# Vision tower kernel: the order of the first microseconds, from the taps' transfer to the second gray picture

## Chip, cores and metric

One core of one Trainium2 chip. The metric is device time in microseconds of one execution. Three runs of the kernel before gave a median of 251.41 us (251.34 to 252.23).

## What is computed

Eight images of 3x256x256 are each turned to gray and convolved with two 3x3 Scharr filters; the mean of the two absolute answers is a matrix of 256x256 per image, whose rows are the tokens. One attention head with biases and a causal mask follows, a residual and a layernorm, then a layer of 8 experts (top 1, at most 320 tokens each) with a residual and a layernorm.

```
gray  = einsum('bchw,c->bhw', x, (0.2989, 0.587, 0.114))
edges = conv(gray, scharr (2 filters), padding='SAME')
h     = (|edges_x| + |edges_y|) / 2                      # [8, 256, 256]
h     = layernorm(h + softmax(mask(Q K^T / 16)) V)       # Q, K, V = h W^T + b
h     = layernorm(h + moe(h, Wr, W1, W2))                # 8 experts, relu, capacity 320
```

## The kernel before, in words

All five engines run their own hand-written programs, ordered by semaphores (`wait_ge`, `then_inc`). Precision is kept by splitting each operand into a high half, rounded by ScalarE to fp32r, and a low half, the rest, which VectorE makes; a product is then three matmuls (high x high, high x low, low x high).

**Setup.** VectorE writes a row of ones and a block of ones (L905, L906, `still_ready`). The 18 taps come by a DMA from ScalarE's queue (L747), TensorE spreads them over 128 partitions (L1444), VectorE scales them (L908, `half_taps`). From them the banded matrices `band[dx, f]` are made, by which a matmul does the vertical part of the convolution: ScalarE writes the first term of each shift dx (L755), VectorE adds the other four (L896). ScalarE rounds the whole band in one activation (`band_high`, L634), VectorE takes its low half (L927). Picture 0 comes in two halves of 128 rows (L370, L371); VectorE makes gray of each (L915 to L922), ScalarE rounds each (L760, L762), and `gray_low(0)` (L887) is the low half.

**TensorE's program** sets the order: the taps' spreading; `keep_warm(9)`, dummy matmuls of 512 columns (L1439); `setup_keys` (L1283, Wq against Wk with the key bias as an extra column; it waits for `attn_w_in` and `key_bias_in`); `setup_biases` (L1292, L1295; it waits for bqc, `bias_in`); `setup_values` (transposes of Wv, L1304, and the router's mean, L1309); the first convolution in three terms, each for both column halves c (36 matmuls, L1345); `setup_gate` (L1318, L1322); `tokens_as_rows(0)` (L1373). Then the loop over the images i: key projection (L1362, three terms of four), value products (L1274 to L1276), scores (L1399), the convolution of image i+1 (L1345), attention (L1409 to L1417) and its tokens as rows. The convolution of image i+1 waits for `rowc_ready`, the row constants that ScalarE reads from the value products' banks.

**ScalarE's program** starts with the issue of the taps (L747) and of the key bias (L748), a table load that stands ahead of its first activation, the band's first terms, the issue of bqc (L757), and `band_high`. After the first image's edges (L641) it rounds the second gray picture (`gray_high(1)`, L630), then the tokens (L649). In the loop: the keys (`project_keys`, L656), the values (L666), the row constants (L672), the blue plane of image i+2 (L623), the softmax.

**VectorE's program** after the band: gray of picture 0, the low halves, the splits of the key and value weights (L1101 to L1117), `make_gray(1)` (L875, L877), the tokens (`tokens`, L935), `gray_low(1)` (L887), `tokens_low(0)` (L940), the value side (L1126 to L1131, which ends with `setup_ev` for the value products), and then the loop, which begins with `keys_low` (L962).

**SP's queue** issues in this order: Wq (L368), Wk (L369), the two halves of picture 0, Wv, Wr, picture 1, the value biases bvc and bvb, picture 2 (waits for gray of picture 0), picture 3 (waits for `make_gray(1)`), then in the loop four fills of the dispatch table with blank rows (L364), further pictures and the experts' weights. POOL scatters rows into that table (L523) once all fills have landed.

The images' phase lasts to about 115 us, the experts' (L1274 to L1276 again, 320 columns) to the end.

Of the kernel before, what the change touches and what calls it, by code (L numbers as in the profile page):

```python
# [6 lines left out]
P = 128  # L7
# [25 lines left out]
def vit_tower_kernel(  # L33
# [19 lines left out]
    TAPS = 3  # L53
# [13 lines left out]
    with ExitStack() as ctx:  # L67
# [17 lines left out]
        one_row = sb("one_row", [1, P])  # L85
        half_taps = sb("half_taps", [P, TAP_COLS])
# [143 lines left out]
        late_z_ready = sem("late_z_ready")  # L230
        spare_rows_ready = sem("spare_rows_ready")
# [100 lines left out]
        def _(sp):  # L332
# [34 lines left out]

            sp.dma_start(wq[:, :, :], Wq.rearrange("(p c) d -> p c d", c=DC)).then_inc(attn_w_in, 16)  # L368
# [251 lines left out]
        def _(act):  # L620
# [11 lines left out]
            def band_high():  # L632
                act.wait_ge(band_ready, 2)
                act.activation(band_hi[:, :, :, :], band[:, :, :, :], ACT.Copy).then_inc(band_hi_ready, 1)  # L634
# [103 lines left out]
            def split_high(n):  # L738
# [4 lines left out]
                if e >= 2:  # L743
# [3 lines left out]
            act.dma_start(taps[:, :], bass.AP(scharr.tensor, 0, [[0, 1], [1, TAP_COLS]])).then_inc(taps_in, 16)  # L747
            act.dma_start(wk[:, :, D:D + 1], bk.rearrange("(p c o) -> p c o", c=DC, o=1),  # L748
                          allow_slow_non_contiguous=True).then_inc(key_bias_in, 16)
            act.wait_ge(scaled_ready, 1)  # L750
# [7 lines left out]
            band_high()  # L758
# [10 lines left out]
            gray_high(1)  # L769
            tokens_high(0)  # L770
            act.wait_ge(setup_ev, 1)
            for i in range(B):
                if 1 <= i < L:
                    gray_high(i + 1)
                project_keys(i)
                project_values(i)
                row_constant(i)
                if i + 2 < B:
                    scale_blue(i + 2)
                elif i < L:  # L780
                    split_high(0)
                if i == L:
                    break
                if i >= 2:
                    norm_lone(i - 2)
                probs(i)
                edges(i + 1, 0)
                if i == L - 1:
                    split_high(1)
                if i >= 1:  # L790
                    route_exp(i - 1)
                prob_t(i)
                edges(i + 1, 1)
                tokens_high(i + 1)
                if i >= 1:
                    norm_rows(i - 1)
# [62 lines left out]
        def _(dve):  # L859
# [31 lines left out]
            def make_band(dx):  # L891
                dve.wait_ge(part_ready, dx + 1)
                for dy in range(1, TAPS):
                    for f in range(2):
                        tap = (f * TAPS + dy) * TAPS + dx
                        ins = dve.scalar_tensor_tensor(band[:, dx, f, :], tap_mask[:, dy], half_taps[:, tap:tap + 1],  # L896
                                                       band[:, dx, f, :], ALU.mult, ALU.add)
                        if dx < TAPS - 1 or dy < TAPS - 1:
                            step(ins)
                        else:  # L900
                            ins.then_inc(band_ready, 1)
                    if dy < TAPS - 1:
                        settle()
# [22 lines left out]
            dve.wait_ge(band_hi_ready, 1)  # L926
# [192 lines left out]
            make_gray(1)  # L1119
            for c in range(DC):  # L1120
                tokens(0, c)
            gray_low(1)
# [9 lines left out]
                              ALU.subtract).then_inc(setup_ev, 1)  # L1132
            dve.wait_ge(pool_const, 3)
            for i in range(L):
# [4 lines left out]
                keys_low(i)  # L1139
                if i >= 1:  # L1140
                    residual(i - 1)
# [127 lines left out]
        def _(pe):  # L1269
# [56 lines left out]
            def convolve(b, c, terms=range(3)):  # L1326
# [6 lines left out]
                for t in terms:  # L1333
# [5 lines left out]
                    for s in range(SC):  # L1339
                        if b == c == t == 0:  # L1340
                            pe.wait_ge(gray_hi_ready if s else first_gray_ready, 1)
                            pe.wait_ge(band_hi_ready, 1)
# [6 lines left out]
                if 2 in terms:  # L1349
# [96 lines left out]
            keep_warm(9)  # L1446
            setup_keys()
            setup_biases()
            setup_values()
            for t in range(3):  # L1450
# [187 lines left out]
```

## Time and profile before

| | |
|---|---|
| median of three runs | 251.41 us |
| the profiled execution | 251.09 us |
| its span, first to last instruction | 249.3 us |
| TensorE busy, matmul | 232.7 us (93%) |
| VectorE busy | 183.8 us (74%) |
| ScalarE busy | 151.6 us (61%) |
| POOL busy | 98.1 us (39%) |
| mean granted TensorE clock | 0.987 |
| chain that ended last: TensorE | 75% |
| the same: transfers, VectorE, issue, POOL | 5% each |

The span runs from the first to the last instruction of the core; the time of the execution is 1.8 us more. Busy time is the time in which an engine has an instruction in work; on TensorE ends are modelled and instructions overlap, so the distance of two starts is the better measure of one. The chain of waits is followed back from the last instruction to what released each step, and its rows give the start and the length of each piece.

### The profile page before, as it was taken

Reading aid. Unit: us, or ns where it says so; the run is one execution under the profiler, and the core shown is the slowest. Engines: PE = TensorE matmul, PEld = TensorE weight load, DVE = VectorE, ACT = ScalarE, POOL = GpSimd, SP = SyncE. Lnnn points to the kernel's source line nnn. Section 1 sums busy time; section 2 is a strip of 40 time slices with the busy share of each in tenths; the row PEclk is TensorE's granted clock in tenths of the full one; section 3 lists DMA queues with packets and bytes.
Section 4 is the critical chain, followed back from the end, with each engine's and each line's share of the span. In section 5 each row is a group of like instructions: output and inputs, shape, how many; then the busy total and the mean of one; then the engine's idle time right before and its main releaser. Section 6 shows DMA issues by size and latency. Waiting matters only on the chain.

```text
span 249.3 us, 4995 instructions
## 1 busy us (share of the span) xinstructions
PE 232.7 (93%) x1673; PEld 223.1 (89%) x1673; DVE 183.8 (74%) x557; ACT 151.6 (61%) x354; POOL 98.1 (39%) x169
## 2 busy tenths in 40 slices
PE   6999999999999999878799999999999999999940
PEld 5899999999999998647799999999999999999940
DVE  4885697887979799786456796749967678779540
ACT  5336567787877786465665477656775758656100
POOL 7000227584665658438100020156260332513662
PEclk9999999999999999999999999999999999999995
DMA  5939563174896020201499919257092460100100
GB/s 175 289 100 304 137 206 135 38 233 148 246 378 224 2 83 15 68 0 43 118 338 293 383 56 313 68 164 261 0 300 93 140 229 3 45 2 24 35 4 0
DMA packets 28378, 35.48 MB, mean 142 GB/s; under 512 B 2780, under 2 KB 25291, under 8 KB 28354
## 3 DMA queue, kind: packets, MB, share of 16 engines
q1 hardware_dynamic: 26144, 31.71, 39.9%
q0 software_dynamic: 1792, 3.47, 3.9%
q8 instruction: 13, 0.21, 0.3%
q14 instruction: 11, 0.09, 0.1%
q10 hardware_dynamic: 418, 0.00, 0.1%
HBM read 26.97 MB, written 9.47 MB: 146 GB/s over the span
## 4 chain that ended last, share of the span: by engine, by line
PE 75%; DMA 5%; DVE 5%; issue 5%; POOL 5%; ACT 2%; POOLq 1%; ACTq 0%; SPq 0%; DVEq 0%
PE bank L1274 14%; PE bank L1276 14%; PE bank L1275 14%; PE bank L1345 14%; PE bank L1399 4%; PE bank L1362 4%; POOL out_dram L573 3%; DMA bqc<-in_L_attn_bq_dram 2%; PE bank L1524 2%; DMA dispatched<-trow,slot 2%; PE bank L1574 2%; PE bank L1415 1%; PE bank L1373 1%; PE bank L1417 1%; PE bank L1416 1%
## 5 line engine op out<-in xcount | busy, mean ns | idle before, releaser
L1191 DVE SCALAR_TENSOR_TENSOR h_lo<-bank,h_hi 128x320 fp32r<-128x320 f32 x58 | 28.3, 488 | 27.4 <-ACT h_hi L817 24.8
L817 ACT ACTIVATE h_hi<-bank 128x320 fp32r<-128x320 f32 x58 | 25.3, 436 | 35.4 <-PE bank L1276 35.4
L573 POOL DMA_INDIRECT out_dram<-tokens_mem,images x24 | 28.0, 1168 | 37.9 <-ACT tokens_mem L834 17.1
L1274 PE MATMUL bank<-einT_hi,w_hi 128*128 128x320 f32 x128 | 40.6, 317 | 0.6 <-DVE einT_lo L1183 0.3
L1275 PE MATMUL bank<-einT_lo,w_hi 128*128 128x320 f32 x128 | 39.5, 308 | 0.0
L1276 PE MATMUL bank<-einT_hi,w_lo 128*128 128x320 f32 x128 | 39.5, 308 | 0.0
L947 DVE TENSOR_TENSOR w_lo<-w_raw,w_hi 128x1024 fp32r<-128x1024 f32 x32 | 38.8, 1214 | 0.0
L1274 PE MATMUL bank<-h_hi,w_hi 128*128 128x320 f32 x112 | 35.2, 314 | 0.1
L1276 PE MATMUL bank<-h_hi,w_lo 128*128 128x320 f32 x112 | 34.6, 309 | 0.0
L1275 PE MATMUL bank<-h_lo,w_hi 128*128 128x320 f32 x112 | 34.6, 309 | 0.0
L745 ACT ACTIVATE w_hi<-w_raw 128x1024 fp32r<-128x1024 f32 x32 | 33.7, 1052 | 0.0
L1274 PEld LDWEIGHTS bank<-einT_hi,w_hi 128*128 128x128 f32 x128 | 24.0, 188 | 1.8 <-DVE h_lo L1191 0.7
L567 POOL TENSOR_TENSOR yrstd<-yve,minus_half 128x3 f32<-128x3 f32 x6 | 5.3, 885 | 47.8 <-DVE yve L1222 47.8
L1275 PEld LDWEIGHTS bank<-einT_lo,w_hi 128*128 128x128 f32 x128 | 24.1, 188 | 0.0
L1276 PEld LDWEIGHTS bank<-einT_hi,w_lo 128*128 128x128 f32 x128 | 24.0, 188 | 0.0
L1274 PEld LDWEIGHTS bank<-h_hi,w_hi 128*128 128x128 f32 x112 | 21.0, 188 | 0.3 <-issue 0.3
L1275 PEld LDWEIGHTS bank<-h_lo,w_hi 128*128 128x128 f32 x112 | 21.0, 188 | 0.0
L1276 PEld LDWEIGHTS bank<-h_hi,w_lo 128*128 128x128 f32 x112 | 21.0, 188 | 0.0
L523 POOL DMA_INDIRECT dispatched<-trow,slot x16 | 17.0, 1064 | 8.8 <-issue 5.7
L641 ACT ACTIVATE tokens_mem<-bank 128x512 f32<-128x512 f32 x16 | 9.6, 598 | 9.0 <-PE bank L1345 8.8
L1274 PE MATMUL bank<-w_hi 128*128 128x274 f32 (+2 forms) x50 | 14.5, 291 | 0.3 <-DVE w_lo L1191 0.3
L1345 PE MATMUL bank<-w_hi 128*128 128x260 f32 x96 | 14.8, 291 | 0.0
(231 smaller groups left out, 577.3 us busy)
## 6 DMA issues: line engine op xcount, KB each, us to landing
w_raw<-in_L_ffn_W_dram SPq DMA_DIRECT2D x16, 1024.0 KB, 7.8
images<-in_x_dram SPq DMA_DIRECT2D x7, 768.0 KB, 4.8
dispatched<-blank SPq DMA_DIRECT2D x4, 645.0 KB, 8.6
images<-dispatched SPq DMA_DIRECT2D x9, 258.0 KB, 7.2
out_dram<-lone SPq DMA_DIRECT2D x8, 256.0 KB, 7.6
images<-in_x_dram SPq DMA_DIRECT2D x2, 384.0 KB, 5.1
images<-dispatched SPq DMA_DIRECT2D x9, 64.5 KB, 7.1
out_dram<-tokens_mem,images POOLq DMA_INDIRECT x24, 2.5
```

Source lines behind the costliest of these rows:

```text
L523: pool.indirect_dma_start(dispatched, bass.IndirectOffsetOnAxis(ap=slot[:, b % TR, s:s + 1], axis=0), trow[:, b % TR, s, :], None, bounds_ ...
L573: pool.indirect_dma_start(out_rows, bass.IndirectOffsetOnAxis(ap=ein[0:n, e, j, D + 1:D + 2].bitcast(U32), axis=0), z[0:n, e % 2, j, :], N ...
L745: act.activation(w_hi[:, e % 2, c], w_raw[:, e % 2, c], ACT.Copy).then_inc(w_hi_ready, 1)
L817: act.activation(hidden_halves(n)[0], bank[n % 2][:, 0:CAP], ACT.Relu).then_inc(h_hi_ready, 1)
L947: dve.tensor_tensor(w_lo[:, e % 2, c], w_raw[:, e % 2, c], w_hi[:, e % 2, c].bitcast(F32), ALU.subtract).then_inc(w_lo_ready, 1)
L1191: dve.scalar_tensor_tensor(lo, bank[n % 2][:, 0:CAP], 0.0, hi.bitcast(F32), ALU.max, ALU.subtract).then_inc(h_ready, 1)
L1274: pe.matmul(to, ah, bh, start=first, stop=False)
L1275: pe.matmul(to, ah, bl, start=False, stop=False)
L1276: return pe.matmul(to, al, bh, start=False, stop=last)
L1345: ins = pe.matmul(acc[:, :, s * (S - REACH):s * (S - REACH) + REACH], half[:, b % 2, s, c * P + dx:c * P + dx + P], of_band[:, dx, :, 2 - ...
L1362: ins = pe.matmul(bank[3][:, c * S:(c + 1) * S], half[:, k, c * P:(c + 1) * P], of_x[:, b % 2, k, :], start=(t == c == k == 0), stop=(t == ...
L1399: ins = pe.matmul(bank[6][:, s * S:s * S + n], half[:, k, s * P:(s + 1) * P], of_x[:, b % 2, k, 0:n], start=(t == s == k == 0), stop=(t == ...
```

## The change

Six edits. The taps' DMA goes from ScalarE's queue to the head of SP's. ScalarE gets a small activation (one partition, 128 columns, a copy of the row of ones into a new tile `still_row`) as its first; its semaphore is awaited by nobody. The band is rounded in three activations, one per shift dx, each as soon as VectorE has made that shift. TensorE does six dummy matmuls instead of nine. The first convolution's first term is cut by row halves s: the six matmuls of the upper half go ahead of `setup_values`, the six of the lower half behind it. The second picture's gray, its rounding and its low half move behind the value side: on ScalarE `gray_high(1)` to a place between `project_keys(0)` and `project_values(0)`, on VectorE `make_gray(1)` to just ahead of the loop and `gray_low(1)` behind `keys_low(0)`.

```diff
--- before.py
+++ after.py
@@ -83,6 +83,7 @@
         TAP_COLS = 2 * TAPS * TAPS
         taps = sb("taps", [1, TAP_COLS])
         one_row = sb("one_row", [1, P])
+        still_row = sb("still_row", [1, P])
         half_taps = sb("half_taps", [P, TAP_COLS])
         rank = sb("rank", [P, SC, E])
         token_id = sb("token_id", [P, T // P], U32)
@@ -228,6 +229,7 @@
         gray_top_ready = sem("gray_top_ready")
         key_bias_in = sem("key_bias_in")
         late_z_ready = sem("late_z_ready")
+        still_row_ready = sem("still_row_ready")
         spare_rows_ready = sem("spare_rows_ready")
         late_probs_ready = sem("late_probs_ready")
         late_turned = sem("late_turned")
@@ -365,6 +367,7 @@
                              blank[:, :].unsqueeze(1).broadcast_to([P, KB, ROW])).then_inc(blanked, 16)
 
 
+            sp.dma_start(taps[:, :], bass.AP(scharr.tensor, 0, [[0, 1], [1, TAP_COLS]])).then_inc(taps_in, 16)
             sp.dma_start(wq[:, :, :], Wq.rearrange("(p c) d -> p c d", c=DC)).then_inc(attn_w_in, 16)
             sp.dma_start(wk[:, :, 0:D], Wk.rearrange("(p c) d -> p c d", c=DC)).then_inc(attn_w_in, 16)
             sp.dma_start(pix[:, 0, :, 0, :], x[0, :, 0:P, :].rearrange("c p d -> p c d")).then_inc(first_pix, 16)
@@ -629,9 +632,9 @@
                     act.wait_ge(conv_done, DC * (b - 1))
                 act.activation(gray_hi[:, b % 2, :, 1:D + 1], red[:, b % 2], ACT.Copy).then_inc(gray_hi_ready, 1)
 
-            def band_high():
-                act.wait_ge(band_ready, 2)
-                act.activation(band_hi[:, :, :, :], band[:, :, :, :], ACT.Copy).then_inc(band_hi_ready, 1)
+            def band_high(dx):
+                act.wait_ge(band_ready, 2 * (dx + 1))
+                act.activation(band_hi[:, dx], band[:, dx], ACT.Copy).then_inc(band_hi_ready, 1)
 
             def edges(b, c):
 
@@ -744,9 +747,10 @@
                     act.wait_ge(h_used, FC * (e - 1))
                 act.activation(w_hi[:, e % 2, c], w_raw[:, e % 2, c], ACT.Copy).then_inc(w_hi_ready, 1)
 
-            act.dma_start(taps[:, :], bass.AP(scharr.tensor, 0, [[0, 1], [1, TAP_COLS]])).then_inc(taps_in, 16)
             act.dma_start(wk[:, :, D:D + 1], bk.rearrange("(p c o) -> p c o", c=DC, o=1),
                           allow_slow_non_contiguous=True).then_inc(key_bias_in, 16)
+            act.wait_ge(row_ready, 1)
+            act.activation(still_row[:, :], one_row[:, :], ACT.Copy).then_inc(still_row_ready, 1)
             act.wait_ge(scaled_ready, 1)
             act.wait_ge(mask_ready, 1)
             for dx in range(TAPS):
@@ -755,7 +759,8 @@
                     ins = act.activation(band[:, dx, f, :], tap_mask[:, 0], ACT.Copy, scale=half_taps[:, tap:tap + 1])
                 ins.then_inc(part_ready, 1)
             act.dma_start(bqc[:, :], bq.rearrange("(p c) -> p c", c=DC)).then_inc(bias_in, 16)
-            band_high()
+            for dx in range(TAPS):
+                band_high(dx)
             act.wait_ge(gray_top_ready, 1)
             act.activation(gray_hi[:, 0, 0, 1:D + 1], red[:, 0, 0], ACT.Copy).then_inc(first_gray_ready, 1)
             act.wait_ge(gray_ready, 1)
@@ -766,13 +771,14 @@
             ins.then_inc(wv_hi_ready, 1)
             for c in range(DC):
                 edges(0, c)
-            gray_high(1)
             tokens_high(0)
             act.wait_ge(setup_ev, 1)
             for i in range(B):
                 if 1 <= i < L:
                     gray_high(i + 1)
                 project_keys(i)
+                if i == 0:
+                    gray_high(1)
                 project_values(i)
                 row_constant(i)
                 if i + 2 < B:
@@ -895,7 +901,7 @@
                         tap = (f * TAPS + dy) * TAPS + dx
                         ins = dve.scalar_tensor_tensor(band[:, dx, f, :], tap_mask[:, dy], half_taps[:, tap:tap + 1],
                                                        band[:, dx, f, :], ALU.mult, ALU.add)
-                        if dx < TAPS - 1 or dy < TAPS - 1:
+                        if dy < TAPS - 1:
                             step(ins)
                         else:
                             ins.then_inc(band_ready, 1)
@@ -923,7 +929,7 @@
                                      ALU.mult, ALU.add).then_inc(gray_ready, 1)
             dve.wait_ge(first_gray_ready, 1)
             gray_low(0)
-            dve.wait_ge(band_hi_ready, 1)
+            dve.wait_ge(band_hi_ready, TAPS)
             dve.tensor_tensor(band_lo[:, :, :, :], band[:, :, :, :], band_hi[:, :, :, :].bitcast(F32), ALU.subtract
                               ).then_inc(band_lo_ready, 1)
 
@@ -1116,10 +1122,8 @@
             for c in range(DC):
                 step(dve.tensor_tensor(wvT_lo[:, c, 0:D], bank[2][:, c * D:(c + 1) * D],
                                        wvT_hi[:, c, 0:D].bitcast(F32), ALU.subtract))
-            make_gray(1)
             for c in range(DC):
                 tokens(0, c)
-            gray_low(1)
             tokens_low(0)
 
             dve.wait_ge(setup_mm, 4)
@@ -1130,6 +1134,7 @@
             link(dve.tensor_copy(wvT_hi[:, :, D:VCOLS], side[:, :, :]))
             dve.tensor_tensor(wvT_lo[:, :, D:VCOLS], side[:, :, :], wvT_hi[:, :, D:VCOLS].bitcast(F32),
                               ALU.subtract).then_inc(setup_ev, 1)
+            make_gray(1)
             dve.wait_ge(pool_const, 3)
             for i in range(L):
                 if i >= 1:
@@ -1137,6 +1142,8 @@
                 if 1 <= i < L:
                     gray_low(i + 1)
                 keys_low(i)
+                if i == 0:
+                    gray_low(1)
                 if i >= 1:
                     residual(i - 1)
                 softmax_max(i)
@@ -1323,7 +1330,7 @@
                                     start=(k == 0), stop=(k == DC - 1))
                 ins.then_inc(setup_mm, 1)
 
-            def convolve(b, c, terms=range(3)):
+            def convolve(b, c, terms=range(3), rows=range(SC)):
 
                 if 0 in terms and b >= 1:
                     pe.wait_ge(gray_hi_ready, b + 1)
@@ -1336,17 +1343,17 @@
                         pe.wait_ge(gray_lo_ready, b + 1)
                     if b == c == 0 and t == 2:
                         pe.wait_ge(band_lo_ready, 1)
-                    for s in range(SC):
+                    for s in rows:
                         if b == c == t == 0:
                             pe.wait_ge(gray_hi_ready if s else first_gray_ready, 1)
-                            pe.wait_ge(band_hi_ready, 1)
+                            pe.wait_ge(band_hi_ready, TAPS)
                         for dx in range(TAPS):
                             first, last = t == dx == s == 0, t == dx == TAPS - 1 and s == SC - 1
                             ins = pe.matmul(acc[:, :, s * (S - REACH):s * (S - REACH) + REACH],
                                             half[:, b % 2, s, c * P + dx:c * P + dx + P],
                                             of_band[:, dx, :, 2 - 2 * s:2 - 2 * s + REACH],
                                             start=first, stop=last, skip_group_check=True)
-                if 2 in terms:
+                if 2 in terms and SC - 1 in rows:
                     ins.then_inc(conv_done, 1)
 
             def project_keys(b):
@@ -1443,11 +1450,15 @@
             pe.wait_ge(taps_in, 16)
             pe.matmul(bank[4][:, 0:TAP_COLS], one_row[:, :], taps[:, :], start=True, stop=True).then_inc(taps_spread, 1)
             pe.wait_ge(still_ready, 1)
-            keep_warm(9)
+            keep_warm(6)
             setup_keys()
             setup_biases()
-            setup_values()
-            for t in range(3):
+            for s in range(SC):
+                for c in range(DC):
+                    convolve(0, c, (0,), (s,))
+                if s == 0:
+                    setup_values()
+            for t in (1, 2):
                 for c in range(DC):
                     convolve(0, c, (t,))
             setup_gate()
```

## Rows read from the trace of the kernel before

**Rows 1.** Chain that ended last, in order of time: start us, us, what.

```profile
0.80 0.55 ACTq L747
...
1.39 0.63 ACTq L748
...
2.11 1.28 ACT L755
...
3.42 5.48 DMA bqc<-in_L_attn_bq_dram
...
8.94 1.05 PE bank L1292 x8
...
11.29 4.52 PE bank L1345 x36
...
17.54 1.55 PE bank L1362 x12
...
19.09 0.33 PE bank L1274
...
28.84 1.43 PE bank L1362 x12
...
30.27 0.13 PE bank L1274
```

**Rows 2.** Timeline, TensorE's dummies and keys: start us, us, engine, line, operation, count.

```profile
2.67 4.21 PE L1439 MATMUL bank<-w_hi 128*128 128x512 f32 x9
...
6.68 2.20 PE L1283 MATMUL bank<-wk,wq 128*128 128x257 f32 x8
...
8.06 0.81 PE L1283 MATMUL bank<-wk,wq 128*128 128x257 f32 x3
...
8.50 0.38 PE L1283 MATMUL bank<-wk,wq 128*128 128x257 f32 x1
```

**Rows 3.** Timeline, SP's queue, the issue of the key weights.

```profile
1.24 0.67 SPq L369 DMA_DIRECT2D wk<-in_L_attn_Wk_dram  x1
```

**Rows 4.** DMA issues by line: KB each, median us from issue to landing.

```profile
dispatched<-blank SPq DMA_DIRECT2D x4, 645.0 KB, 8.6
...
wk<-in_L_attn_Wk_dram SPq DMA_DIRECT2D x1, 256.0 KB, 4.2
...
wk<-in_L_attn_bk_dram ACTq DMA_DIRECT2D x1, 1.0 KB, 4.7
```

**Rows 5.** Timeline, VectorE and ScalarE, before the first convolution.

```profile
2.78 0.18 DVE L908 TENSOR_SCALAR half_taps<-bank 128x18 f32<-128x18 f32 x1 [1.20 <-PE bank L1444]
...
3.40 0.40 ACT L755 ACTIVATE images<-images,half_taps 128x132 f32<-128x132 f32 x1
...
8.78 0.42 ACT L760 ACTIVATE w_hi<-red 128x256 fp32r<-128x256 f32 x1
...
10.70 0.97 DVE L927 TENSOR_TENSOR w_lo<-images,w_hi 128x792 fp32r<-128x792 f32 x1
```

**Rows 6.** Timeline, from the first tokens to the second convolution.

```profile
16.34 0.62 ACT L630 ACTIVATE w_hi<-red 128x512 fp32r<-128x512 f32 x1
...
16.99 0.69 DVE L887 TENSOR_TENSOR w_lo<-red,w_hi 128x512 fp32r<-128x512 f32 x1
...
17.61 0.69 DVE L940 TENSOR_TENSOR w_lo<-xT,w_hi 128x512 fp32r<-128x512 f32 x1
...
18.77 0.20 DVE L1131 TENSOR_TENSOR w_lo<-side,w_hi 128x36 fp32r<-128x36 f32 x1
...
20.86 0.69 ACT L666 ACTIVATE val<-bank 128x272 f32<-128x272 f32 x2 [0.83 <-PE bank L1276]
...
21.43 0.42 ACT L672 ACTIVATE rowc<-bank,bias_dot 128x1 f32<-128x1 f32 x2
...
21.96 0.79 PEld L1345 LDWEIGHTS bank<-w_hi 128*128 128x128 f32 x6
```

**Rows 7.** Timeline, POOL, the first scatter into the table.

```profile
41.74 1.22 POOL L523 DMA_INDIRECT dispatched<-trow,slot  x1 [0.64 <-issue]
```

## The prediction

> **What bounds the kernel now.** I read the page's chain shares first, then the chain in order of time, then the timeline of the first 22 us, since all edits lie there. Up to 8.94 us the chain runs through ScalarE's queue and a transfer: the taps' issue, the key bias' issue, ScalarE's table load, and then 5.48 us of waiting for bqc, the query bias, whose issue stands behind that load [rows 1]. From 8.94 us the chain is TensorE without a hole to the end of the first images: each step follows the one before at once, and the last image steps repeat the same pieces [rows 1]. So the reader is to see two things. What ends the start is bqc's landing, and whatever time TensorE gains before about 22 us is passed on by a chain of matmuls that nothing else interrupts. A gain off that chain is worth nothing.
>
> There are also small holes behind the first convolution: the key projection of image 0 takes 1.55 us where that of image 1 takes 1.43, and the first value product takes 0.33 where its later twin takes 0.13 [rows 1]. Together 0.32 us, and both are VectorE's doing: the low half of the tokens starts at 17.61, behind gray_low(1) at 16.99, and the last of the value side (L1131) ends at 18.97, just ahead of that product [rows 6].
>
> **The change part by part.** Queue of the taps. ScalarE's queue loses one issue, 0.59 us from 0.80 to the next at 1.39, and the table load moves from 2.11 to about 1.52, ending at 2.80 instead of 3.39 [rows 1]. The extra small activation ahead of it is one more instruction of ScalarE: between 0.21 (a 128x1 one, two in 0.42 [rows 6]) and 0.40 (a 128x132 one [rows 5]); I take 0.3, so ScalarE is free at 3.1. The scaled taps are there at 2.96 [rows 5], if the taps land as before; the first band activation moves from 3.40 [rows 5] to 3.1, and bqc's issue with it, from 3.42 [rows 1] to 3.1. Nobody waits for the small activation's own semaphore.
>
> On SP's queue everything behind the taps is issued one slot later, about 0.55 us (what ScalarE's queue took for the same transfer [rows 1]): the weights Wq and Wk, both halves of picture 0, Wv, Wr, picture 1, and the bvc and bvb issues. Wk was issued at 1.24 [rows 3] and took 4.2 [rows 4], 5.44; now about 6.0. The key bias goes the other way, 1.39 plus 4.7 was 6.09 [rows 1, 4], now about 5.5. Six dummy matmuls instead of nine: nine began at 2.67 and the keys at 6.68 [rows 2], 0.446 each, so six end at 5.35 and the keys start with Wk at 6.0 instead of 6.68.
>
> Clock. A dummy moves 512 columns in 0.446 us, the lower of the two clock levels (1.2 GHz), although the profile's granted clock says 1.00 there; a convolution matmul moves 260 columns in 4.52 / 36 = 0.126 us [rows 1], the upper level (2.4 GHz). The last key records are 0.22 apart ((8.50 - 8.06) / 2), but all seven steps from 6.68 to 8.50 take 1.82 [rows 2], so the first of them still ran low, and the clock rose at about 7.3. Keys from 6.0 with the rise at the same moment: three records at 0.44, five at 0.22, end 8.4 instead of 8.72. bqc, with its old 5.48, lands at 8.6; the bytes that SP issues later stand partly behind it now, so I take 8.5. From below, the shortest of the transfers of that stretch took 4.2 [rows 4], which gives 7.3; from above, it lands at 8.9 as before because the 16 engines hand out the same bytes. The bias matmuls start at the later of 8.4 and bqc: 8.5, a gain of **0.44**; ends 0 and 1.15 (keys wholly at 0.22 from 6.0 end at 7.8).
>
> The Trainium skill ("DMA: Bandwidth & Descriptors", Issuing engines are not separate DMA queues) says that transfers from all engines run on the same 16 DMA engines and that another queue saves only the time of the issuing. The rows fit it: transfers issued around 1.3 by two queues both land at 5.4 to 6.1. By that rule alone the taps' move is worth at most ScalarE's 0.59.
>
> Band rounded per shift. One copy of 792 columns becomes three of 264, the last about 0.42 (as L760's 256 columns [rows 5]) behind the last band instruction. The band's waits do not reach TensorE: the bias and value matmuls fill it until 11.29 [rows 1], while the upper gray half was rounded at 9.20 [rows 5]. Cover about 2 us, so nothing. If it were gone, the three copies would cost 0.4 more of ScalarE than one.
>
> Value weights inside the first convolution. The same instructions in another order; the six matmuls of the upper half (6 x 0.126 = 0.75) go first and need data of 9.20, when TensorE comes to them at about 10.0. Nothing. Behind them the turned value weights are 0.75 later, about 11.5; VectorE is in band_lo until 11.67 and has the key weights after that [rows 5]. gray_low(0) and band_lo are needed only from the second term on. Nothing again.
>
> Second gray picture later. VectorE's two passes over 128x512 (0.69 each, as L887 [rows 6]), ScalarE's rounding (0.62) and gray_low(1) leave the stretch of the first tokens. Both holes go, **0.32**. What is late next is the row constant of image 0, on which TensorE's second convolution waits. In the old times: tokens' low half starts near 17.4 (ScalarE has no gray copy between), the value side ends 1.36 later (18.97 - 17.61 [rows 6]) at 18.76, the picture is gray at 20.14, rounded at 20.8. The value products, 0.32 earlier, are ready at 20.54 instead of 20.86 [rows 6], so ScalarE comes 0.26 late to them. Before, the constants ended at 21.85 and the second convolution's first load went at 21.96 [rows 6]: 0.11 of slack. A new stall of **0.15**; ends 0 and 0.4. keys_low stands behind the picture too, at 20.14; its two passes of 256 columns (0.42 each, taken as L760's) end near 21.0, and of the scores, which run from 20.54 to 21.64, only the last third, from about 21.3, needs them. Queued behind make_gray(1) on SP are picture 3 and the first two table fills, 4 to 5 us later, at about 20; a fill lands 8.6 after issue [rows 4], and the first scatter goes at 41.74 [rows 7]. Nothing, cover over 10 us.
>
> **Sum.** 0.44 + 0.32 - 0.15 = 0.61 us off. The profiled execution took 251.09 (span 249.3), so 250.5; the median of the runs, 251.41, stands 0.32 above it, so **250.8**. A measurement of this kernel can tell about 0.5%, 1.26 us, from no change: below 250.15 is faster, above 252.67 slower.
>
> **The rivals.** First, *more is gained*: bqc lands with the faster transfers (7.3) and the clock rises earlier, so the keys end at 7.8, and no stall comes at the row constant: 1.15 + 0.32 = 1.47, 249.9. For it: SP's bytes get out of bqc's way. Against: the keys' two low-clock steps are in the trace. Chance 0.15.
>
> Second, *the start does not move*: the taps on SP land later or Wk's slot costs as much as the dummies save, bqc lands at 8.9. Then 0.32 - 0.15 to 0.4 of stall is left: 251.2 to 251.5. The change's first part does nothing then. For it: all transfers of that stretch share the engines. Chance 0.2.
>
> Third, *slower by the clock*: six dummies leave TensorE idle from 5.35 to 6.0, where it had no idle time before the keys. 
>
> **Chances.** Forecast 0.6, own range 250.2 to 251.2; the rivals 0.15, 0.2, 0.05. The range 249.8 to 251.7 takes in the first two rivals and the spread of the old runs. Only the first is faster by over 0.5%, with some of the forecast's lower edge: 0.17; slower 0.05; within 0.5% 0.78.
>
> **What would show it.** Right: the table load starts near 1.5 and bqc's issue near 3.1; the keys' first record near 6.0 and the bias matmuls near 8.5; the first convolution's end 0.4 to 0.5 earlier; no wait at L1362 and L1274 of image 0; a hole of 0.1 to 0.2 ahead of the second convolution with ScalarE's row constant as its releaser; from there on the same steps, shifted by 0.6. Wrong: key records 0.44 apart to the end, convolution matmuls at 0.22, a bias start still at 8.9, a hole above 0.5 at the second convolution, or picture 3 or the fills awaited by anyone.

## The result and the profile after

The changed kernel took 250.39 us in the median of ten runs, beside 251.50 for the kernel before in ten runs taken with it: a ratio of 0.9953, 95% interval 0.9935 to 0.9971. By the ratio that is 1.2 us, and within what I had called no change (0.5%), on the faster side of it. The forecast of the time was 250.8, 0.4 us too long. One of the ten runs took 800.97 us, a single execution that nothing on record explains; the nine others have a median of 250.03, and the ratios here and below are of means that leave out executions more than 1.5% above the fastest of their kernel. Its profiled execution has a span of 248.1 us against 249.3.

From the page of the kernel after, the span, the busy time of TensorE, and the shares of its chain:

```profile
span 248.1 us, 4992 instructions
...
PE 231.7 (93%) x1670; PEld 222.3 (90%) x1670; DVE 184.4 (74%) x557; ACT 152.2 (61%) x357; POOL 97.9 (39%) x169
...
PE 77%; DVE 7%; issue 5%; POOL 5%; DMA 3%; ACT 1%; POOLq 1%; SPq 0%; DVEq 0%; ACTq 0%
```

The same shares were 75% and 5% for TensorE and transfers before: the wait for bqc is gone from the chain. The chain of the kernel after, in order of time (start us, us, what):

```profile
0.79 1.20 DMA taps<-in_L_tok_scharr_dram
...
2.71 2.86 PE bank L1446 x6
5.56 2.21 PE bank L1290 x8
7.77 0.79 PE bank L1299 x8
...
9.00 0.84 PE bank L1352 x6
9.85 0.44 PE bank L1311 x4
...
10.63 3.77 PE bank L1352 x30
...
16.13 1.43 PE bank L1369 x12
17.56 0.23 PE bank L1281
...
20.56 3.71 PE bank L1352 x30
```

Read it against [rows 1]. The chain is now TensorE from the taps' landing on, without a hole. The bias matmuls (L1299) stand at 7.77 where they stood at 8.94. The chain counts a piece from the end of the one before it; by its own start, which the table below uses, the first bias matmul stands at 7.61. The key projection (L1369) is back to 1.43 from 1.55, and the first value product (L1281) takes 0.23 instead of 0.33. From the last matmul of the first convolution (it starts at 14.12, before 15.52) to the first of the second (20.40, before 22.03) it is 6.28 us instead of 6.51.

The timeline of the kernel after, for ScalarE, its queue and SP's at the start, and for ScalarE and TensorE's loads at the second convolution:

```profile
1.47 1.28 ACT L753 ACT_TABLE_LOAD   x1 [1.47 <-PEq L1636]
...
2.77 0.31 ACT L753 ACTIVATE still_row<-one_row 1x128 f32<-1x128 f32 x1
...
2.97 0.41 ACTq L761 DMA_DIRECT2D bqc<-in_L_attn_bq_dram  x1
2.97 0.49 SPq L374 DMA_DIRECT2D images<-in_x_dram  x1
...
5.36 2.41 PE L1290 MATMUL bank<-wk,wq 128*128 128x257 f32 x8
...
18.71 0.63 ACT L633 ACTIVATE w_hi<-red 128x512 fp32r<-128x512 f32 x1 [0.21 <-DVE red L883]
...
19.24 0.67 ACT L669 ACTIVATE val<-bank 128x272 f32<-128x272 f32 x2
...
19.80 0.42 ACT L675 ACTIVATE rowc<-bank,bias_dot 128x1 f32<-128x1 f32 x2
...
20.33 0.79 PEld L1352 LDWEIGHTS bank<-w_hi 128*128 128x128 f32 x6
```

The table load, the small activation and bqc's issue are within 0.15 of where the forecast put them (1.52, 0.3, 3.1). The constants end at 20.22 and the second convolution's first load goes at 20.33: the slack of 0.11 is the old one [rows 6], so the stall that I had reckoned did not come. What I had not seen stands in the transfers of the kernel after (KB each, us from issue to landing):

```profile
wk<-in_L_attn_Wk_dram SPq DMA_DIRECT2D x1, 256.0 KB, 3.4
...
wk<-in_L_attn_bk_dram ACTq DMA_DIRECT2D x1, 1.0 KB, 2.8
bqc<-in_L_attn_bq_dram ACTq DMA_DIRECT2D x1, 1.0 KB, 3.5
```

They took 4.2, 4.7 and 5.5 before [rows 4, 1]. Wk landed at 5.0 (1.63 + 3.4), earlier than before though issued later.

### The profile page after: what moved, and what is told of

Same layout as the page of the kernel before. It is cut to its first block, busy times and chain, and to the rows that moved or that the text cites. A ratio compares the mean times of both kernels' runs of the same rounds, so it can differ in the third digit from the quotient of the medians.

```text
span 248.1 us, 4992 instructions
## 1 busy us (share of the span) xinstructions
PE 231.7 (93%) x1670; PEld 222.3 (90%) x1670; DVE 184.4 (74%) x557; ACT 152.2 (61%) x357; POOL 97.9 (39%) x169
## 4 chain that ended last, share of the span: by engine, by line
PE 77%; DVE 7%; issue 5%; POOL 5%; DMA 3%; ACT 1%; POOLq 1%; SPq 0%; DVEq 0%; ACTq 0%
PE bank L1281 14%; PE bank L1283 14%; PE bank L1282 14%; PE bank L1352 13%; PE bank L1406 4%; PE bank L1369 4%; POOL out_dram L576 3%; PE bank L1535 2%; DMA dispatched<-trow,slot 2%; PE bank L1585 2%; PE bank L1380 1%; PE bank L1422 1%; PE bank L1446 1%; PE bank L1423 1%; PE bank L1424 1%
## 5 line engine op out<-in xcount | busy, mean ns | idle before, releaser
L1281 PE MATMUL bank<-einT_hi,w_hi 128*128 128x320 f32 x128 | 40.6, 317 | 0.6 <-DVE einT_lo L1190 0.3
L1281 PE MATMUL bank<-h_hi,w_hi 128*128 128x320 f32 x112 | 35.2, 315 | 0.1
L1281 PEld LDWEIGHTS bank<-einT_hi,w_hi 128*128 128x128 f32 x128 | 24.0, 188 | 1.8 <-DVE h_lo L1198 0.7
L1281 PEld LDWEIGHTS bank<-h_hi,w_hi 128*128 128x128 f32 x112 | 21.0, 188 | 0.3 <-issue 0.3
L1281 PE MATMUL bank<-w_hi 128*128 128x274 f32 (+2 forms) x50 | 14.5, 290 | 0.3 <-DVE w_lo L1198 0.3
L1352 PE MATMUL bank<-w_lo,w_hi 128*128 128x260 f32 x96 | 14.8, 291 | 0.0
```

The lines of the kernel that those rows point to most:

```text
L1281: pe.matmul(to, ah, bh, start=first, stop=False)
L1352: ins = pe.matmul(acc[:, :, s * (S - REACH):s * (S - REACH) + REACH], half[:, b % 2, s, c * P + dx:c * P + dx + P], of_band[:, dx, :, 2 - ...
```

## The experiments

Twelve kernels ran, in three groups of four, each beside the kernel before on its chip. The traces tell more here than the times, whose ratios have intervals of 0.2 to 0.4% either way; but each trace is one execution. So the table has the starts (us) of TensorE's first key, first bias matmul, first and last matmul of the first convolution and first of the second, in the profiled execution of each, and the ratio to the kernel before. Only two ratios stand apart from the changed kernel's without an overlap of the intervals: undo_taps from the kernel run again on the same chip, by 0.0003, and no_dummies from both runs of it.

| kernel | keys | biases | conv. 1 first | last | conv. 2 | ratio (95%) |
|---|---|---|---|---|---|---|
| before | 6.68 | 8.94 | 11.14 | 15.52 | 22.03 | |
| after | 5.36 | 7.61 | 8.87 | 14.12 | 20.40 | 0.9953 (0.9935 to 0.9971) |
| same | 5.37 | 7.22 | 8.84 | 14.10 | 20.39 | 0.9941 (0.9916 to 0.9965) |
| undo_taps | 6.67 | 10.22 | 12.64 | 20.61 | 26.90 | 0.9997 (0.9968 to 1.0025) |
| undo_dummies | 6.21 | 7.94 | 9.20 | 14.44 | 20.73 | 0.9977 (0.9955 to 0.9999) |
| undo_gray | 5.38 | 8.79 | 10.05 | 15.31 | 21.82 | 0.9949 (0.9926 to 0.9973) |
| no_small_act | 5.37 | 8.33 | 9.69 | 14.94 | 21.23 | 0.9960 (0.9930 to 0.9991) |
| no_split | 5.37 | 7.65 | 9.95 | 14.32 | 20.61 | 0.9959 (0.9938 to 0.9981) |
| one_band | 5.59 | 7.89 | 9.26 | 14.51 | 20.79 | 0.9954 (0.9931 to 0.9978) |
| no_dummies | 5.13 | 8.69 | 10.18 | 15.42 | 21.71 | 1.0017 (0.9979 to 1.0056) |
| before_taps_on_sp | 6.63 | 8.37 | 11.23 | 15.60 | 22.11 | 0.9969 (0.9945 to 0.9993) |
| before_bqc_early | 6.66 | 8.78 | 10.87 | 15.22 | 21.98 | 0.9980 (0.9959 to 1.0001) |
| dummy_first | 5.63 | 8.05 | 9.33 | 14.59 | 20.88 | 0.9949 (0.9927 to 0.9971) |
| dummy_first_bqc_on_sp | 5.62 | 8.88 | 10.13 | 15.39 | 21.67 | 0.9946 (0.9924 to 0.9968) |

**The changed kernel again.** No edit.

> The changed kernel once more, unaltered. Profiled before it gained 1.64 us up to the second convolution and gave 0.5 of it back in images 3 to 6, where VectorE's score operation started 0.17 late beside a small POOL operation and the tokens' sum then waited for POOL's blue sum. If that is a chance tie between two engines at one memory port, this second profile differs from the first in the image loop (start of the last image's tokens-as-rows at 94.49, by 0.3 or more) while the first 20 us agree within 0.05. If it is fixed by the program, both profiles agree throughout. Time 249.8 to 251.1.

The starts agree to 0.03 up to the second convolution (20.39 and 20.40), but for the biases: they are 0.39 earlier here, as the clock rose earlier, and TensorE then waits 0.22 for the rounded upper gray half, so that nothing of it is left at the first convolution. The image loop does not agree: the eighth convolution starts at 87.45 here, at 87.99 in the first profile and at 89.12 before. So 1.67 us are kept to that point here and 1.13 there. The place where they part, in the loop's pass over image 3, in the timeline of the first profile and then of this one:

```profile
53.93 0.20 POOL L513 TENSOR_TENSOR onehots<-onehots,onehot 128x8 bf16<-128x8 bf16 x1
...
54.14 0.29 DVE L993 CUSTOM_DVE_ANT_0 tokens_mem<-bank,causal 128x128 f32<-128x128 f32 x1 [0.49 <-PE bank L1406]
...
58.84 1.33 POOL L534 TENSOR_TENSOR red<-red,images 128x512 f32<-128x512 f32 x1 [1.22 <-DVE red L888]
...
59.69 0.76 DVE L941 TENSOR_TENSOR xT<-tokens_mem 128x256 f32<-128x256 f32 x1 [0.57 <-ACT tokens_mem L644]
```

```profile
53.91 0.20 POOL L513 TENSOR_TENSOR onehots<-onehots,onehot 128x8 bf16<-128x8 bf16 x1
53.93 0.29 DVE L993 CUSTOM_DVE_ANT_0 tokens_mem<-bank,causal 128x128 f32<-128x128 f32 x1 [0.32 <-PE bank L1406]
...
58.64 1.33 POOL L534 TENSOR_TENSOR red<-red,images 128x512 f32<-128x512 f32 x1 [1.22 <-DVE red L888]
...
59.67 0.58 DVE L941 TENSOR_TENSOR xT<-tokens_mem 128x256 f32<-128x256 f32 x1 [0.76 <-ACT tokens_mem L644]
```

VectorE's score operation (L993) starts 0.02 behind the start of a POOL operation of 0.20 here and behind its end there: 0.2 later. Everything on VectorE follows by 0.2, POOL's addition of the blue plane (L534) too, and the tokens' sum (L941), which takes 0.42 alone, ends 0.28 behind the end of that addition in both (60.45 behind 60.17, 60.25 behind 59.97), 0.20 later in the first profile. The next key projection then starts at 60.70 instead of 60.51. In the next two images it repeats. That the two engines share a path to memory is what the rows suggest, and no run took it apart.

The other profiles say to what the tie belongs. From the start of the second convolution to that of the eighth it takes 67.06 to 67.09 us in five of the fourteen profiles (the kernel before and all four on the chip of this run: same, undo_taps, undo_dummies, undo_gray) and 67.49 to 67.60 in the nine others, the first profile of the changed kernel and both single edits of the kernel before among them. So the half microsecond is no price of the change: one program shows both values, and on each chip of the three groups every profile shows the same one. How many of the unprofiled runs paid it isn't known.

In this second profile 0.3 went elsewhere: the last scattered rows took 5.04 us to land (4.71 before, 4.53 in the first profile), and its last instruction is as early as the first profile's to 0.05.

**The taps back on ScalarE's queue.**

```
-            sp.dma_start(taps[:, :], ...)        # head of SP's queue
+            act.dma_start(taps[:, :], ...)       # head of ScalarE's queue
```

> Only the taps' DMA goes back to the head of ScalarE's queue. Queue theory: the key bias is issued 0.6 later and the table load starts at 2.1 again, bqc is issued near 3.7 (behind load and small activation) and lands at 7.2 or later; bias matmuls from 7.8 or later instead of 7.4, time 0.3 to 1.0 longer than the changed kernel's. Rival (the dummies alone made the start earlier): bias matmuls still at 7.4 to 7.6, time the same within 0.2.

The chain of this kernel (its profiled execution took 255.9 us):

```profile
1.38 5.15 DMA wk<-in_L_attn_bk_dram
...
6.67 3.77 PE bank L1290 x8
10.43 1.50 PE bank L1299 x8
```

The key bias, issued 0.14 behind Wk, took 5.15 us where it takes 2.8 if issued ahead of Wq. TensorE had nothing from the last dummy's end at about 5.4 until 6.67, matmuls stayed at the lower level, and the keys took 3.77 instead of 2.21. The first convolution's matmuls ran low until 18.7 us. The profiled execution is one of two of the 13 that took 255.8, and the ratio without these two is 0.9997, against 0.9941 for the changed kernel on the same chip: with the taps here nothing of the change's gain can be measured. The queue theory was right in its direction and too small: it had 0.3 to 1.0 us, the ratios say 1.4, with about 0.9 either way. In the profiled execution most of the loss is the clock's and not the queue's; what the eleven others lost by, no trace shows.

**Nine dummies.** `keep_warm(6)` to `keep_warm(9)`.

> Nine dummy matmuls instead of six. The dummies end near 6.85 instead of 5.56, the keys start there and the bias matmuls follow at 8.6 if the clock rises as before. Dummies theory: convolution end 1.0 to 1.3 later than in the changed kernel, time 0.6 to 1.2 longer. Rival (bqc's landing alone decided, the dummies nothing): same as the changed kernel.

The clock rose during the seventh dummy here (its successor starts 0.36 behind it, the next 0.23, where low ones are 0.43 apart), so nine ended at 6.2, not 6.85, and the second convolution is 0.33 later than in the changed kernel. By the ratios the three dummies are worth about 0.4% (0.9977 beside 0.9941 on the same chip, the intervals overlapping a little), some 0.9 us, inside the 0.6 to 1.2 expected, though the trace shows 0.33. With the clock of the kernel before, whose nine all ran low, the trace would have shown more.

**The second gray picture early again.**

```
+            make_gray(1)                  # VectorE, ahead of tokens(0, c)
+            gray_low(1)                   # behind them
+            gray_high(1)                  # ScalarE, ahead of tokens_high(0)
```

> Only the second gray picture goes back to its old places on both engines. The two holes at the first key projection (1.55 instead of 1.43) and the first value product (0.33 instead of 0.23 or less) come back: second convolution 0.2 to 0.35 later than in the changed kernel, time 0.0 to 0.4 longer. Rival (the gray's place is worth nothing since the rest of the side moved too): no difference at the second convolution within 0.05.

The two holes are back, as its chain shows:

```profile
17.32 1.56 PE bank L1367 x12
18.88 0.33 PE bank L1279
```

The key projection takes 1.56 and the first value product 0.33. From the last matmul of the first convolution to the second convolution it takes 6.51, as before the change; all ten kernels with the gray picture late, whatever their start, take 6.28 or 6.29. The term is 0.23, and it is the cleanest number of the study. In the ratio it can't be seen (0.9949 beside 0.9941). That the second convolution starts at 21.82, 1.4 late, is mostly the clock: all eight key records ran low, 0.43 apart, to 8.8.

**Without the small activation.**

```
-            act.wait_ge(row_ready, 1)
-            act.activation(still_row[:, :], one_row[:, :], ACT.Copy).then_inc(still_row_ready, 1)
```

> The changed kernel without the small activation on the row of ones; the taps stay on SP's queue. Theory of mine (the load follows ScalarE's last DMA issue): the table load still starts near 1.5, the first band activation at 2.98 and bqc's issue at 2.97, nothing changes, time the same within 0.2. Rival (the load waits with the activation it stands ahead of): the load starts at 2.9 to 3.0 when the scaled taps are ready, the band's first activation near 4.2, gray top rounded 1.2 later, bqc issued at 4.2, time 0.8 to 1.5 longer.

Neither theory held. The timeline of ScalarE, its queue and TensorE, and then bqc's row among the transfers:

```profile
1.83 1.28 ACT L757 ACT_TABLE_LOAD   x1 [1.83 <-POOL images L438]
...
3.15 0.36 ACTq L759 DMA_DIRECT2D bqc<-in_L_attn_bq_dram  x1
...
8.33 1.05 PE L1297 MATMUL bank<-bqc,wk 128*128 128x1 f32 x8 [0.39 <-DMA bqc<-in_L_attn_bq_dram]
```

```profile
bqc<-in_L_attn_bq_dram ACTq DMA_DIRECT2D x1, 1.0 KB, 5.1
```

The load waits for the band's mask (`mask_ready`, the second of the two waits ahead of it), not for the taps: 1.83 instead of 1.47. bqc's issue is 0.18 later, and that puts it behind the second half of picture 0 on SP (2.97): it takes 5.1 instead of 3.5, lands 1.8 later, and TensorE waits 0.39 for it. So the small activation is worth 0.15 of ScalarE's time and, by the order of two issues, up to 0.4 on TensorE.

**The value weights ahead of the first convolution.** The loop over `s` around `setup_values` is undone.

> The value weights are turned ahead of the whole first convolution again. Theory: the changed kernel reaches them at 9.6, after Wv's landing near 9.0 (3.50 + 5.5); without the six upper matmuls ahead TensorE would be there at 8.8 and wait for Wv and Wr until 9.1 to 9.3, so the first convolution's last matmul is 0.1 to 0.7 later (14.2 to 14.8 instead of 14.1) and the time 0 to 0.6 longer. Rival (my prediction's nothing): last matmul at 14.1 as before, time the same within 0.2.

TensorE's next work after the bias matmuls starts 0.66 behind the last group of them here and 0.45 in the changed kernel: the transposes, at 9.12, wait about 0.2 for Wv, which lands at 9.0. From the first bias matmul to the convolution's last it is 6.67 instead of 6.51. The split is worth 0.16: not nothing, because TensorE now gets there before Wv.

**The band in one rounding.** `band_high` once, with `band_ready` at 6, over all of `band`.

> The band is rounded in one activation of 792 columns again. It would run from about 7.57 to 8.43 on ScalarE and the gray top's rounding behind it, from 8.4 instead of 8.36: first convolution matmul at 8.9 instead of 8.84, time the same within 0.15 (prediction's nothing). Rival (the cover is gone now that TensorE is there by 8.8): the rounding of gray top moves by 0.4, convolution and everything behind it 0.3 to 0.4 later.

The taps landed 0.22 later in this execution, and all after it too. With that off, the upper gray half is rounded at 8.37 (8.59 - 0.22), the changed kernel's 8.36. The three roundings are worth nothing, as forecast. What the late taps did cost is bqc: ScalarE issued it at 3.19, 0.22 behind picture 0's second half, it took 4.7 us, and TensorE waited for it although the keys were done:

```profile
7.89 1.05 PE L1298 MATMUL bank<-bqc,wk 128*128 128x1 f32 x8 [0.35 <-DMA bqc<-in_L_attn_bq_dram]
```

So the changed kernel's start still hangs on when the taps land, since bqc's issue follows them.

**No dummies.** `keep_warm(6)` is left out.

> No dummy matmul between the taps' spreading and the keys. Clock theory (the upper level comes after a stretch of work, at a moment that differs between executions, and idle time puts it off): keys from about 5.05 at the low level, 0.43 apart, through all eight, biases and at least part of the first convolution (0.217 a matmul instead of 0.126) low too; second convolution 0.5 to 3 later than 20.4 and some executions 3 us or more longer. Rival (the clock rises at the same moment whatever TensorE did): keys from 5.05 and everything up to 0.3 earlier than in the changed kernel, time 249.6 to 250.4.

The timeline's key matmuls in this kernel, in the changed kernel run again, and in the one with the gray picture early:

```profile
5.13 3.77 PE L1290 MATMUL bank<-wk,wq 128*128 128x257 f32 x8 [2.42 <-DMA wk<-in_L_attn_Wk_dram]
```

```profile
5.37 2.01 PE L1290 MATMUL bank<-wk,wq 128*128 128x257 f32 x8
```

```profile
5.38 3.57 PE L1288 MATMUL bank<-wk,wq 128*128 128x257 f32 x8
```

Without dummies the twelve runs fall in two groups, six from 251.1 to 251.7 and six from 253.8 to 255.4, and the granted clock at the start reads 1.00 in all three of these. The times fit the clock theory, but the trace is of the quicker group (251.44 us): it has every key at the lower level, and so has undo_gray, whose six dummies ran. That the slower six ran low into the convolution is argued from the trace of undo_taps (255.9 us, low until 18.7); no trace of the group was kept, and the table's ratio leaves four of the six out. The last two rows show the other half: with the same six dummies the keys may take 2.0 or 3.6 us. The steps between starts (0.43 at the lower level, 0.22 at the upper) put the rise at 7.3 in the kernel before, at 6.4 in the changed one, at 5.6 in its second profile, and beyond 8.6 in undo_gray.

**The kernel before with the taps on SP's queue.**

> The kernel before with one edit: the taps' DMA at the head of SP's queue. Order theory (a small transfer of ScalarE's queue lands early if it is issued ahead of the large ones of SP and late if behind): the key bias, issued at 0.8 ahead of Wq's packets, lands in 2.8 to 2.9 instead of 4.7; the table load starts at 1.8, bqc is issued at about 3.15, behind the second half of picture 0 (2.97), and still takes 4.7 to 5.1, landing near 8.2; bias matmuls start when the keys end, 8.1 to 8.7 by the clock, instead of 8.94, time 0.2 to 0.8 less than before. Rival (landing depends on the bytes in flight alone): bqc takes 5.5 as before and the key bias over 4.

The key bias took 2.9, bqc, issued at 3.15, took 5.1; the bias matmuls start with the keys' end at 8.37. Of that 0.57 nothing is left at the convolution, because Wv took 6.8 us in this execution and TensorE waited 0.61 for it. So the landings went as the order theory had them, and the rival (bqc in 5.5, the key bias over 4) is out. The ratio, 0.9969, has this one edit at about 0.8 us, 0.2 to 1.4 by its interval.

**The kernel before with bqc right behind the key bias.**

> The kernel before with one edit: bqc is issued right behind the key bias on ScalarE's queue, at about 2.05, ahead of both halves of picture 0. Order theory: it lands before 6.5 and TensorE does not wait for it; bias matmuls follow the keys at 8.1 to 8.7 instead of 8.94. The table load moves to 2.5 and the band with it, by 0.4, so gray top is rounded near 9.6, still ahead of the convolution's 10.9; second convolution 0.2 to 0.8 earlier. Rival (nothing but bytes): bqc lands at 7 or later.

The timeline's two issues, and bqc's row among the transfers:

```profile
1.96 0.58 SPq L370 DMA_DIRECT2D images<-in_x_dram  x1
...
2.02 0.80 ACTq L750 DMA_DIRECT2D bqc<-in_L_attn_bq_dram  x1
```

```profile
bqc<-in_L_attn_bq_dram ACTq DMA_DIRECT2D x1, 1.0 KB, 5.4
```

It landed at 7.4, which is the rival's number. bqc stood 0.06 behind the issue of picture 0's first half, and that half lands at about 7.2. This corrects the theory: in these traces a small transfer lands about when the large one issued last ahead of it does, on whichever queue that was. Wk (5.4) and the key bias (6.1) in the kernel before, the first picture half (6.8) and bqc (6.5) in the changed one, Wv (9.1) and bqc (8.9) in the kernel before are such pairs. The match is within 0.7 us in these, and 1.1 in undo_taps (Wk 5.4, key bias 6.5). The Trainium skill ("DMA: Bandwidth & Descriptors", Issuing engines are not separate DMA queues) has it that transfers of all engines interleave on the same DMA engines, and that issuing from several engines saves only the time of issuing. The rows agree with the first and go beyond the second: the order in which they are issued moved the same key bias from 2.8 to 5.2 us.

The edit gained little all the same: the second convolution starts 0.05 earlier, where 0.2 to 0.8 was expected. The first convolution's last matmul is 0.30 earlier. But bqc's issue held ScalarE's table load back from 2.11 to 2.91, the band and VectorE's work behind it came later (its last pass of the second gray picture at 15.55 instead of 14.77), and from that matmul to the second convolution it takes 6.76 instead of 6.51.

**One dummy ahead of the taps' matmul,** and the same with bqc on SP's queue between Wk and picture 0.

> The changed kernel with one more dummy matmul, put ahead of the taps' spreading, so that TensorE works from 1.65 instead of 2.13. Clock theory: the upper level comes earlier or as early in each execution, so that fewer executions have keys at 0.43 to the end; keys start at 5.4, spread of the runs smaller and the median 0 to 0.4 less than the changed kernel's. Rival (the clock rises at its own moment): spread and median as the changed kernel's within 0.2.

> As the kernel with the first dummy, and bqc issued on SP's queue between Wk and picture 0, so that its landing no longer hangs on which queue issues first near 2.97. bqc lands before 6.5 in every execution; picture 0 lands 0.4 later (7.2 and 7.9), the second half's gray perhaps 0.1 later, Wv near 9.4, where TensorE comes at 9.6. If late landings of bqc cost the changed kernel anything in the median, 0 to 0.4 less than it; if not, the same or 0.1 more.

The clock rose at about 7.1 in the one and after 8.6 in the other, no earlier than without that dummy, which also held the taps' matmul up by 0.2 (2.36). bqc on SP landed at 5.3, 0.2 behind Wk, the large transfer ahead of it, and well ahead of need. Ratios 0.9949 and 0.9946: neither differs from the changed kernel. No version beat it.

## Why the prediction was right, and where it was off

The direction, the range (249.8 to 251.7) and "within 0.5%" held; the terms did not all. That the number came so near is partly luck: at the second convolution the gain was 1.63 us and not 0.61, and a part of it was lost again for reasons that the forecast did not have. Without the run of 800.97 us the median, 250.03, would even lie beyond the 250.15 that I had set as the edge of no change.

**The start, forecast 0.44, measured 1.33** (8.94 to 7.61), and 1.40 at the convolution's last matmul. The step that was mis-sized is the landing: I kept the old durations, 4.2 for Wk and 5.48 for bqc, and set 7.3 as bqc's earliest. Both depend on what is issued ahead. With the key bias ahead of Wq and bqc level with the second picture half they took 3.4 and 3.5: Wk was there at 5.0, bqc at 6.5. The keys then waited for the dummies, not for Wk, and started at 5.36 instead of my 6.0; bqc held up nobody. The second part was the clock: I let it rise at the same moment as before, 7.3, and it rose at 6.4. That moment differs between executions, so I should have carried it in the range. The Trainium skill ("TensorE: Matmul & The Clock Gate", Part 1) calls it run-variable, and the two traces of the same program, 6.4 and 5.6, agree. How the 0.89 us beyond the forecast divide between the landings and the clock no run separates.

**The holes behind the first convolution, forecast 0.32 less a stall of 0.15, measured 0.23 net.** Only 0.22 of the 0.32 came: the first value product takes 0.23 and not its twin's 0.13, and it starts at 17.40, 0.05 behind the end of the value side (L1135), as it did before (19.02 behind 18.97), so by the rows it still waited for it. The stall was an artefact of adding up full durations: the value side's last operation and make_gray, and the rounding and the values' reading, overlap by 0.1 each, and ScalarE came to the values at 19.24, with TensorE's product ending at 19.18.

**The costs at nothing.** The band's roundings, the table fills (issued at 19.1, the first scatter at 40.12 after 41.74) and the SP issues behind the taps cost nothing. The split was worth 0.16 and not nothing. The small activation earned more than its own 0.3: I had put the table load's whole move, 2.11 to 1.52, down to the queue, but with the taps on SP and no such activation the load starts at 1.83 (no_small_act, before_taps_on_sp), because it waits for the mask. The move to 1.47 is the activation's.

**What was missing** is the give-back: 1.63 us at the second convolution were 1.26 at the end. In the first profile it went in the image loop (1.13 left at the eighth convolution), where a tie between VectorE and POOL fell the other way than in the trace of the kernel before, from image 3 on; that is a difference between executions and no effect of the edits, as its appearance in both single edits of the kernel before shows. In the second the loop kept 1.67 and the landing of the last scattered rows took 0.3 of it. I wrote that nothing interrupts that chain; it does not stop, yet its pieces near VectorE's and POOL's big operations have no slack. The rival *more is gained* had the better mechanism: bqc landed early, the clock rose earlier and no stall came (1.15 as its bound at the start, 1.33 measured), and the median missed its 249.9 by 0.5. The slower rival's mechanism is real, as the keys at the lower level in undo_taps and the six slower runs of no_dummies suggest, but with six dummies and Wk in time TensorE was idle for nothing before the keys.

## What to carry to other kernels

A small transfer that something waits for belongs ahead of the large ones, on any queue: here it landed about with the large transfer issued just before it, and 0.18 us of issue decided 1.8 us of landing (bqc at 6.5 in the changed kernel, at 8.3 without the small activation). When an issue order changes, the durations of the old trace are no longer prices. Dummy matmuls should end when the first real operand lands. Later costs their own time (0.33 us for three); earlier cost 2 to 4 us in half of the runs without any. A difference in a loop that no edit touches should be looked for in every profile before it is put down to the change.

## What the hardware showed that I had not expected

The moment at which TensorE goes from 1.2 to 2.4 GHz moved between 5.6 and past 8.6 us over executions with six dummies from 2.65 us on (the levels are read from the steps of the keys, 0.43 and 0.22). Between the profiles of same and undo_gray it is worth 1.6 us at the first bias matmul and 1.2 at the first convolution's last, while the granted clock read 1.00 throughout. And a VectorE sum (L941 in the changed kernel) that takes 0.42 us alone took 0.46 to 0.80 beside POOL's addition, its end 0.28 or 0.29 behind POOL's in the last three such places of all fourteen profiles.
